# A decoder layer on one core: every engine's list of calls in another order

## What is computed

```python
x = layernorm(x + self_attention(x))      # causal; scores mix two forms of K through W_cross, shift_weights, gate
x = layernorm(x + cross_attention(x, ctx))# ctx is 375 rows, keys masked by a 1x1x112x375 mask
gate, y = fp4_linear(x, w_gate), fp4_linear(x, w_up)          # 704 wide
x = layernorm(x + fp4_linear(silu(gate) * y, w_down))

def fp4_linear(x, w):                     # both sides to FP4 (E2M1) and back, a scale for each 16 values
    return einsum("bsk,nk->bsn", fp4_quant_dequant(x), fp4_quant_dequant(w))
```

## Time and profile before

| | us |
|---|---|
| three runs | 636.06, 634.17, 629.39 |
| median | 634.17 |
| the profiled execution | 636.34 |
| its span | 634.5 |

### The profile page before, as it was taken

How to read it: one execution, slowest core, us unless ns; L and a number is a source line. 1 busy time by engine, 2 the same in 40 slices (tenths; PEclk the granted TensorE clock), 3 DMA queues, 4 the chain that set the end, 5 groups by cost and what they waited for, 6 DMA issues and landing times.

```text
span 634.5 us, 16557 instructions
## 1 busy us (share of the span) xinstructions
PE 550.2 (87%) x5724; PEld 354.5 (56%) x5724; DVE 511.8 (81%) x1444; ACT 285.9 (45%) x671; POOL 177.7 (28%) x251
## 2 busy tenths in 40 slices
PE   3677688769989999999999998898999998887885
PEld 2445345546566665766565656564665764454543
DVE  3387778867898989899998997567989996887894
ACT  1242235446545455554555545444454554443412
POOL 7014122325131332424141323141232424211211
PEclk9698899899999999999999998888999999997999
DMA  8265453544353462626363634435362625320000
GB/s 245 45 206 174 119 145 126 157 112 141 106 171 105 109 173 76 190 84 175 89 179 91 181 94 132 153 108 163 97 179 70 192 81 149 88 84 17 24 8 26
DMA packets 75934, 77.16 MB, mean 122 GB/s; under 512 B 13068, under 2 KB 67404, under 8 KB 75852
## 3 DMA queue, kind: packets, MB, share of 16 engines
q1 hardware_dynamic: 73612, 73.75, 40.9%
q10 hardware_dynamic: 2240, 2.35, 1.3%
HBM read 39.89 MB, written 27.00 MB: 105 GB/s over the span
## 4 chain that ended last, share of the span: by engine, by line
PE 48%; DVE 25%; issue 11%; DMA 7%; ACT 4%; POOL 3%; SPq 2%; DVEq 0%; POOLq 0%; ACTq 0%
PE misc L2248 15%; PE misc L2234 7%; DVE junk L1431 5%; PE score L2164 4%; PE xpv L2223 3%; PE prob L2173 3%; PE misc L2276 3%; PE apv L2211 2%; PE prob L2179 2%; PE misc L2289 2%; DVE xden L1470 2%; DMA xden<-xoT 2%; DMA xQ<-xq_dram 2%; DVE qt L1348 2%; DMA hqT<-in_mask 2%
## 5 line engine op out<-in xcount | busy, mean ns | idle before, releaser
L1431 DVE CUSTOM_DVE_ANT_0 junk<-score,maskbias 112x375 bf16<-112x375 f32 x256 | 129.1, 543 | 37.2 <-PE score L2164 36.0
L932 ACT ACTIVATE xP<-prob 128x448 f32<-128x448 f32 (+1 forms) x192 | 93.9, 541 | 56.7 <-PE prob L2179 56.5
L2248 PE MATMUL misc<-wguT,xqT 128*128 128x352 f32 x224 | 81.8, 494 | 1.9 <-ACT xqT L892 1.1
L2164 PE MATMUL score<-xK,xQ 64*128 64x375 f16 x256 | 44.4, 334 | 21.9 <-DVE xmax L1431 20.2
L741 POOL TENSOR_TENSOR move_a<-mT,eye 128x448 bf16<-128x448 bf16 x32 | 36.3, 1154 | 78.6 <-ACT mT L892 78.6
L765 POOL TENSOR_TENSOR rstd<-veps,half 128x1 f32<-128x1 f32 (+1 forms) x44 | 28.0, 637 | 101.4 <-DVE veps L1506 101.4
L2276 PE MATMUL misc<-ctxT_s,xwkT_s 128*128 128x375 f32 x128 | 51.9, 530 | 4.2 <-DVE bq_s L1390 4.2
L2248 PEld LDWEIGHTS misc<-wguT,xqT 128*128 128x128 f32 x224 | 40.0, 196 | 26.3 <-issue 9.7
L741 POOL TENSOR_TENSOR move_x<-mT,eye 128x448 bf16<-128x448 bf16 x32 | 33.1, 1040 | 77.1 <-ACT mT L892 77.1
L761 POOL TENSOR_TENSOR aattT<-anum,aden 128x224 f32<-128x224 f32 x16 | 11.0, 684 | 155.3 <-DVE aden L1470 132.7
L2248 PE MATMUL misc<-xwvT_s,ctxT_s 128*128 128x256 f32 (+1 forms) x192 | 50.3, 394 | 3.1 <-DVE ak_parts L1450 2.1
(11 more groups left out here) (158 smaller groups left out, 1100.5 us busy)
## 6 DMA issues: line engine op xcount, KB each, us to landing
xk_dram<-xk_parts SPq DMA_DIRECT2D x64, 192.0 KB, 3.2
xK<-xk_dram SPq DMA_DIRECT2D x16, 768.0 KB, 4.5
ctxT_s<-in_ctxT SPq DMA_DIRECT2D x15, 375.0 KB, 3.5
aq_dram<-aq_parts SPq DMA_DIRECT2D x64, 64.0 KB, 2.5
ak_dram<-ak_parts SPq DMA_DIRECT2D x64, 64.0 KB, 2.3
aQ<-aq_dram SPq DMA_DIRECT2D x16, 256.0 KB, 2.9
aK<-ak_dram SPq DMA_DIRECT2D x16, 256.0 KB, 2.9
xq_dram<-xq_parts SPq DMA_DIRECT2D x64, 64.0 KB, 2.1
```

Of the source, the lines that this page charges most:

```text
L932: act.activation(xP[0:KEYS[c], g % 2, c], prob[m][0:KEYS[c], 0:GH * S].rearrange("p (h q) -> p h q", h=GH), ACT.Exp).then_inc(probs.taken[ ...
L1431: dve.tensor_tensor_reduce(junk[:, m], score[m][0:S, 0:SC], maskbias[:], 1.0, -3.0e38, ALU.add, ALU.max, xmax[:, b.par, h // (2 * GH), h / ...
L2164: pe.matmul(score[m[a]][:, 0:SC], xQ[rows_, b.par, at, :], xK[rows_, b.par, at, 0:SC], start=True, stop=True).then_inc(scores.full[m[a]], 1)
L2248: mm = pe.matmul(misc[m][0:rows_, 0:cols], actT(c), weightT(c), start=(c == 0), stop=(c == DT - 1))
```

## The change

The lists of all five engines are written in another order: in `ramp`, in `slot` and in `drain`. The multiset of calls of every engine and part is the same, and no helper is touched; the lists of bank uses follow PE's new order. Of the positions, 138 of 219 differ in PE's ramp, 8 of 50 in its slot, 36 of 109 in its drain; on DVE 204 of 222, 24 of 63 and 132 of 191. `-` is before and `+` after. The core of the diff (about 1,600 lines in all; the hunks of ACT, POOL and SP move calls in the same manner):

DVE, ramp, first hunk:

```diff
             def ramp():
                 masks()
+                quant_weight(0, 0)
+                quant_weight(0, 1)
                 mixed_bias()
                 q_lo(at[-2], at[0])
+                quant_weight(0, 2)
                 k_lo(at[-2], at[0])
-                quant_weight(0, 0)
-                quant_weight(0, 1)
-                quant_weight(0, 2)
+                quant_weight(0, 3)
                 k_lo(at[-1], at[1])
-                q_lo(at[-1], at[1])
-                quant_weight(0, 3)
                 quant_weight(0, 4)
                 quant_weight(0, 5)
                 quant_weight(0, 6)
                 ctxk_lo(at[-1], at[0], 0)
+                q_lo(at[-1], at[1])
                 quant_weight(0, 7)
+                quant_weight(0, 8)
+                max_self(at[-1], at[0], 0)
                 k_lo(at[0], at[2])
-                quant_weight(0, 8)
                 quant_weight(1, 0)
-                max_self(at[-1], at[0], 0)
                 max_self(at[-1], at[0], 1)
+                quant_weight(1, 1)
+                max_self(at[-1], at[0], 2)
+                quant_weight(1, 2)
+                max_self(at[-1], at[0], 3)
+                quant_weight(1, 3)
                 ctxk_lo(at[-1], at[0], 1)
-                max_self(at[-1], at[0], 2)
-                max_self(at[-1], at[0], 3)
-                ctxk_lo(at[0], at[1], 0)
-                quant_weight(1, 1)
-                quant_weight(1, 2)
-                ctxk_lo(at[0], at[1], 1)
-                quant_weight(1, 3)
                 quant_weight(1, 4)
                 quant_weight(1, 5)
+                bias_out()
                 quant_weight(1, 6)
                 quant_weight(1, 7)
                 quant_weight(1, 8)
                 quant_weight(2, 0)
-                bias_out()
-                invert(at[0], 0)
                 quant_weight(2, 1)
                 q_lo(at[0], at[2])
+                invert(at[0], 0)
...
```

DVE, ramp, a later part (slots 0 to 2):

```diff
                 max_self(at[1], at[2], 1)
-                quant_weight(4, 2)
-                quant_weight(4, 3)
                 max_self(at[1], at[2], 2)
-                quant_weight(4, 4)
                 quant_weight(4, 5)
+                quant_weight(4, 6)
                 max_self(at[1], at[2], 3)
-                quant_weight(4, 6)
+                max_cross(at[1], at[1], 0)
+                ctxk_lo(at[1], at[2], 0)
                 quant_weight(4, 7)
-                quant_weight(4, 8)
-                quant_weight(5, 0)
-                max_cross(at[1], at[1], 0)
                 max_cross(at[1], at[1], 1)
                 max_cross(at[1], at[1], 2)
+                quant_weight(4, 8)
+                k_lo(at[2], at[4])
+                quant_weight(5, 0)
+                max_cross(at[1], at[1], 3)
...
                 max_cross(at[1], at[1], 7)
-                quant_weight(5, 8)
                 quant_weight(6, 0)
+                max_self(at[2], at[3], 0)
                 xq_lo_(at[1], at[2])
+                max_self(at[2], at[3], 1)
                 quant_weight(6, 1)
-                invert(at[0], 1)
-                max_self(at[2], at[3], 0)
+                max_self(at[2], at[3], 2)
+                q_lo(at[2], at[4])
+                max_self(at[2], at[3], 3)
                 quant_weight(6, 2)
                 quant_weight(6, 3)
+                invert(at[0], 1)
                 ctxk_lo(at[2], at[3], 0)
-                max_self(at[2], at[3], 1)
-                max_self(at[2], at[3], 2)
-                max_self(at[2], at[3], 3)
-                quant_weight(6, 4)
-                q_lo(at[2], at[4])
-                quant_weight(6, 5)
-                quant_weight(6, 6)
-                quant_weight(6, 7)
                 max_cross(at[2], at[2], 0)
...
```

DVE, slot:

```diff
                 if f:
                     quant_h(i, f, 1, 0)
                     quant_h(i, f, 0, 4)
+                    quant_h(i, f, 1, 1)
+                    quant_h(i, f, 1, 2)
                 max_cross(i, c, 6)
-                if f:
-                    quant_h(i, f, 1, 1)
                 residual_self(i, a)
                 if f:
-                    quant_h(i, f, 1, 2)
+                    quant_h(i, f, 1, 3)
                 moments(i, a, 0, "A.o", 0)
+                ctxk_lo(i, kv, 0)
+                moments(i, a, 0, "A.o", 1)
                 if f:
                     quant_h(i, f, 0, 5)
-                moments(i, a, 0, "A.o", 1)
-                if f:
-                    quant_h(i, f, 1, 3)
                 moments(i, a, 0, "A.o", 2)
                 invert(ct, 1)
-                ctxk_lo(i, kv, 0)
+                if f:
+                    quant_h(i, f, 1, 4)
                 ctxk_lo(i, kv, 1)
-                if f:
-                    quant_h(i, f, 0, 6)
-                    quant_h(i, f, 1, 4)
                 max_cross(i, c, 7)
                 if xo:
                     residual_cross(i, xo)
                 if f:
...
```

PE, slot:

```diff
                 front(i, fr, "v")
                 bias_self(i, 1)
                 if ft:
-                    turn_hq(i, ft, "hT1", range(4, IC))
                     turn_hq(i, ft, "hT0", range(4))
                 scores_self(i, a, 1)
+                if ft:
+                    turn_hq(i, ft, "hT1", range(4, IC))
                 pv_cross(i, p, 0, 0)
                 pv_cross(i, p, 0, 1)
                 turned_cross(i, p, 0, 2)
@@ -2605,11 +2601,11 @@
                 turned_cross(i, p, 1, 2)
                 if f:
                     gate_up(i, f, "up", 1)
+                ctx_k(i, kv, 0)
                 scores_cross(i, c, 5)
                 pv_cross(i, p, 1, 0)
                 pv_cross(i, p, 1, 1)
                 pv_cross(i, p, 1, 2)
-                ctx_k(i, kv, 0)
                 scores_cross(i, c, 6)
                 project_self(i, a)
```

DVE, drain:

```diff
                 max_self(at[14], at[15], 0)
                 max_self(at[14], at[15], 1)
+                layernorm(at[10])
                 max_self(at[14], at[15], 2)
                 max_self(at[14], at[15], 3)
-                layernorm(at[10])
                 quant_x(at[10], 0)
                 quant_x(at[10], 1)
+                max_cross(at[14], at[14], 0)
                 quant_x(at[10], 2)
-                max_cross(at[14], at[14], 0)
                 quant_x(at[10], 3)
...
-                moments(at[15], at[12], 1, "X.o", 2)
-                quant_h(at[15], at[11], 0, 7)
-                quant_h(at[15], at[11], 0, 8)
                 quant_h(at[15], at[11], 1, 8)
-                invert(at[15], 1)
                 residual_ffn(at[15], at[10])
                 moments(at[15], at[10], 2, "down", 0)
+                invert(at[15], 1)
                 layernorm(at[12])
...
-                residual_ffn(at[16], at[11])
                 moments(at[16], at[11], 2, "down", 0)
                 layernorm(at[13])
                 quant_x(at[13], 0)
                 quant_x(at[13], 1)
-                moments(at[16], at[11], 2, "down", 1)
+                gate_(at[16], at[12], 0)
                 quant_x(at[13], 2)
                 quant_x(at[13], 3)
-                moments(at[16], at[11], 2, "down", 2)
-                gate_(at[16], at[12], 0)
...
```

653 lines of the change are left out of this document (332 added, 321 removed), and 8 rows, old and new, of the table MISC_IN.

## The result

The changed kernel takes 648.64 us (median of 4 executions, 647.96 to 654.37) against 634.64 us for the kernel before on the same chip (4 executions, 629.39 to 636.06): ratio 1.0256, 95% interval [1.0173, 1.0339]. It is slower by 2.6%, clear of noise, and lies above the range of 624 to 645. The profiled execution took 654.37 us, with a span of 652.5.

A forecast was written before the change was run, and what follows sets the result against it. Steady slots were taken to run at PE's pace, both ends as chains where PE and DVE wait for each other. Ramp +0.7, slots +0.7, slot 10 -0.5 and drain +1.5 gave +2.4: 636.6, called 636.5, range 624 to 645.

The forecast's parts named there:

- (a) to (c): Ramp up to about 119 us: start -0.7, bias_out() 0, max_cross(1,1,0) ahead of quant_weight calls +0.7.
- (d): Ramp, 149 to 158 us: about 4 us of quant_weight moved there, covered by DVE's idle time; +0.7, at most +4.
- (i): Slot's end: quant_h(.,0,6) behind max_cross(7) could bring the maximum 0.5 earlier and shorten PE's wait; bound -0.5 a slot.
- (ii): Slot's end: ctxk_lo and quant_h ahead of the moments make the layernorm 1.0 late, stalling PE about 0.7 at turn_x1.
- (iii): Slot: ctx_k(kv,0) ahead of scores_cross(5) and three pv_cross makes the attention numerators' copy 1.0 later, no new wait.
- (iv): Slot: one of PE's two turn_hq calls goes behind scores_self(1); PE has other work there, no cost.
- Slot 10: The slot without an FFN tile: a ctx_k fills idle time of PE there, -0.5.
- The drain: Drain: invert(15,1) after the residual moves project_cross by 1.2, the tail starts later; +1.5, from 0 to +4.
- rival A: Whole kernel faster through the ramp's clock and a shorter wait at turn_max in the slots; 626 us, chance 0.25.
- B: Ramp: DVE owes more than its 6.75 us idle between 147 and 188, so slower; 643 us, chance 0.11.
- C: Slots: a stall of 0.7 to 0.8 at turn_x1 stays in each of ten; +8, 643 us, chance 0.08.
- D: Slots: one more DVE step and POOL step meet and block each other; +6.6, 641 us, chance 0.04.

The follow-up runs named there:

- qh_late: The kernel before with only DVE's quant_h(i,f,0,6) moved behind max_cross(i,c,7) and residual_cross in the slot; 627.96 us, ratio 0.9958.
- ramp_only: The kernel before with the changed ramp lists on all five engines, slot and drain as before; 638.83 us, ratio 1.0121.
- qw_back: ramp_only with DVE's quant_weight (6,4) to (6,8) and (7,0) put back to their old places; 648.39 us, ratio 1.0271.
- sec_c: The kernel before with the changed ramp only from about 161 us on, SP's list old; 643.29 us, ratio 1.0189.
- slot_only: The kernel before with the changed slot lists on all five engines, ramp and drain as before; 637.5 us, ratio 1.0109.
- ctxk_undo: slot_only with PE's ctx_k(i,kv,0) moved back behind pv_cross(1,2); 632.22 us, ratio 0.9997.
- invert_early: The changed kernel with DVE's invert(15,1) put back ahead of residual_ffn(15,10) in the drain; 645.38 us, ratio 1.0222 against before.
- sec_a: The kernel before with the changed ramp only up to about 118 us, plus SP's whole new ramp list; 640.71 us, ratio 1.015.
- tail_b: ramp_only with three places at the ramp's end put back on PE and DVE; 641.36 us, ratio 1.0139 against before.

## Why the prediction was wrong

The forecast was 636.5 and the time 648.64: the sum was 12 us too low. By its steps:

- **(a) to (c), the ramp's start: about right in sum.** Taken: 0.0. The orders are level at 140 us (140.0 and 140.3); against qh_late with its old ramp, at the same half clock, ramp_only is 1.8 behind there. The new wait of DVE at bias_out is 3.32 us (forecast 4.0), the one at max_cross(1,1,0) 4.05 (about 4), PE's wait for bq_s 4.12, the one for aattT 3.65 where it was 2.42. Timeline of DVE, after:

```profile
49.09 0.42 DVE L1394 TENSOR_TENSOR bo_s<-bo_s,misc 112x256 f32<-112x256 f32 x1 [3.32 <-PE misc L2106]
...
96.65 0.55 DVE L1431 CUSTOM_DVE_ANT_0 junk<-score,maskbias 112x375 bf16<-112x375 f32 x1 [4.05 <-PE score L2159]
```

- **(d), from 141 us on: the step that failed.** Taken: +0.7, at most +4 if DVE's debt does not fit. Measured: +8.2 for the ramp at equal clock, most of it here. The number that was set against the loss, 6.75 us of idle DVE between 147 and 188, was beside the point: moving the calls back (qw_back) gained nothing. I had followed how much DVE has to do in the stretch, and not in which order the waiting calls stand at its end: residual_self ahead of up, scores_cross(3,3,3) behind project_self and front. The idle time of an engine covers work only if that work does not stand in front of something that PE waits for. The order of the tail costs 4.3 us by the start of slot 4, in sec_c as in after. Putting three of its places back returned 2.1 of them there and about 1 ± 1 at the end of the kernel.
- **The transfers, "land well before PE reads them": wrong.** PE's waits for xQ went from 1.3 to 6.1 us in sum, the longest 2.96 at 71.4 us.
- **The slot, (i): right for the call alone.** The wait at turn_max was to shrink by 0.5; qh_late alone shows 0.76 to 0.33, worth 3.6 us; the prediction's bound for it was -5. In the changed slot the gain does not come out.
- **(ii), the stall at turn_x1: did not come.** In after turn_x1 has no wait, since PE itself comes there 30.96 us into the slot and not 30.09 as before (slot 6; timeline of PE, after, slot 5):

```profile
259.12 0.41 PE L2284 MATMUL misc<-ident,x 112*128 112x112 f32 x2
...
260.99 0.41 PE L2196 MATMUL misc<-ident,xmax 112*128 112x112 f32 x2
```

- **(iii), ctx_k(kv,0) ahead of scores_cross(5): the second step that failed, costed at nothing, worth +4.1 alone and 3.5 in the changed slot.** The prediction said "no new wait" because DVE comes to the invert about 1 us later as well. Alone, the call makes DVE wait 0.22 and 0.21, and DVE's chain sets turn_max. The right question was which engine's chain ends at turn_max: the wait of 0.84 there was read as room that a stall of PE could use, and it was the sign that DVE had none.
- **(iv), "PE has other work in its place, no cost".** A wait of 0.24 for xP did appear, by way of ACT, which the step did not look at. Taking it away in slot_only gained nothing. But in ctxk_undo PE comes to turned_cross(p,0,2) 0.63 us later in the slot than before, and the trace puts the lost gain of (i) there; the step had no term for it.
- **Slot 10, -0.5 taken: did not come.** It takes 34.78 us in after and 34.49 before.
- **The drain: +1.5 taken, +2.1 ± 0.5 alone.** The size was about right for the part alone; the cause was not. invert's place was not what counted (invert_early); the timelines point to the late pv_cross. The term had no share for the clock: in after the two new waits of 2.40 and 2.03 have half clock behind them.
- **The clock.** It stood in the prediction as a gain of up to 4 us in rival A, and for the loss only beside a stall that did not come. after has 71.7 us at half clock in its profiled execution (its stretches in the windows view), before 47.5; at 0.29 us each that is 7 of the 18 us between the profiles. In after's other three executions it is 52 to 56, where before has 48.8 in the mean, and that is worth 1 to 2 us. So the clock is not the cause of the slower median. Waits of about 2 us often have the slow clock behind them, as in the earlier trace rows, but not always: the same wait at the end of slot 9 has it in before and ramp_only, and none in sec_a (1.77), sec_c and tail_b (1.78), nor has sec_a's 1.98 at 168.96 (clock 1.00 up to 190). The Trainium skill, "TensorE: Matmul & The Clock Gate", section "HAM oscillation — how this bites in real kernels", says that a loop in which PE runs dry pays the slow clock again each time. The slots here show only the other side: with waits of 0.2 to 0.8 they keep 0.98.

Of the rivals, B and C named a loss of about the right sign and the wrong place: qw_back speaks against B, and C's stall never showed. D, the meeting of DVE and POOL, was not tried, but the profiles speak against it: DVE is busy 502.2 us in after and 511.8 before with the same 1444 instructions, so its steps became shorter and not longer. What stays open is some 3 of the ramp's 8 us, and in the slot what eats the gain of (i).

## What to carry to other kernels

Before a call is moved, ask which engine's chain ends last at the next wait: where PE waits 0.8 us for DVE, half a microsecond taken from DVE is won (3.6 us over the kernel), and a matmul of 1.5 us put ahead of what DVE waits for is lost (4.1 us), however idle PE looks. A stretch with idle time does not hide a call that stands in front of something awaited, so compare the order at the end of the stretch, not its sums. Where several orders are changed at once, run the parts by themselves, down to single calls: a gain of 3.6 us from one moved call did not show among the others, and here the best kernel is before with that single call moved. A sum of idle time says what could be gained at most; a section of the new order run with everything else old says what it costs.

## What the runs showed of the chip

- Each us at half clock goes with 0.286 ± 0.012 us of time, over 227 executions, where 0.5 would be the price if PE's work filled it and nothing hid behind a wait. One kernel, before, has 29 to 73 us of it in its 89 executions, which differ by up to 2.3%, more than most of these edits are worth.
- A change of order can call up 20.4 us of half clock in one piece (qw_back, 132 to 153 us) though PE is busy for 15.19 of it. Its four executions have 72 us at half clock in the mean, those of ramp_only 46.
- One and the same wait of PE, 1.78 us at the end of slot 9, is followed at once by 3.4 us at half clock in some profiles (before, ramp_only) and by full clock for 19 us and more in others (sec_c, tail_b).
- Four writes of xq_parts that land in 2.1 to 3.2 us with the load of xK issued 5 us ahead of them (before) took 3.2 to 4.3 with it issued 0.6 us ahead on the same queue (sec_a).
